# Six transformer layers twice over, on one core: the attention's weighted sum with the values as weights, and a new order of all engines

## The chip, the cores and the metric

The kernel runs on one core of one Trainium2 chip. The metric is the device time of one launch in microseconds, the median of several runs. A core has TensorE (matrix multiplication, writes to PSUM only), VectorE, ScalarE, GpSimd (which reaches SBUF, not PSUM), a SyncE queue that issues the transfers, and 16 DMA engines. In the profile they are PE (with PEld for its weight loads), DVE, ACT, POOL and SP.

## The reference, cut to what matters

The program is a residual chain of four phases on a tensor of 4 x 512 tokens by 128 features: a retention attention, a stack of six layers, an RWKV-like mixer, and the same stack again. The change touches the stack alone, which runs twice. All is float32. One layer of it, cut down:

```python
def attn_layer(x, Wqkv, qs, ksc, Wo):          # 16 heads of 64, windows of 32
    q, k, v = split(x @ Wqkv)                  # 128 -> 3 x 1024
    q, k = l2norm(q) * qs, l2norm(k) * ksc     # then rotary tables with a scale
    sim = einsum('bhwie,bhwje->bhwij', bq, look(bk)) * QK_SCALE   # own and previous window: 64 keys
    attn = softmax(where(mask, -max, sim), -1)
    out = einsum('bhwij,bhwje->bhwie', attn, look(bv))
    return out.reshape(b, n, INNER) @ Wo       # 1024 -> 128
def ffn_layer(x, g, bln, W1, b1, W2, b2):
    a, gate = split(layernorm(x) * g + bln @ W1 + b1)   # 128 -> 2 x 341
    return a * gelu(gate) @ W2 + b2
```

Before each layer's parts half of the features are shifted by one token, and each part is added to its input.

## The kernel before, in words

`ffn_stack` works through 96 tiles in each run of the stack: six layers, four sequences (a *group* of four tiles is one sequence in one layer), 128 tokens a tile. With two runs there are 192 tiles and 48 groups. Work is software-pipelined by *slots*: in slot N each engine does, in an order written out by hand (`slot` of each engine's block), one step of several tiles. `at(3)` is tile N-3, `of(2)` is group G-2; T is N mod 4, and steps of a group stand in one of the four kinds of slot. Nothing schedules at run time: each engine issues in its order, and waits on counting semaphores (`wait`).

A tile goes through these steps. GpSimd stages its 128x128 input (`stage`). TensorE projects six chunks of 512 columns, q0, q1, k0, k1 (8 heads each) and v0, v1 (`project`). VectorE multiplies q and k by the rotary tables out of PSUM (`rotate`, two instructions a chunk), ScalarE squares them (`square`) for the norms, GpSimd adds the two products (`rope`) and multiplies by the inverse norm (`unit`). TensorE transposes each of the four chunks (`turn`, 4 transposes), ScalarE copies them out (`keep`). `scores` are 2 x 32 small matmuls. VectorE adds the mask and takes the maximum (`mask_max`), GpSimd subtracts it (`off_max`), ScalarE takes the exponential (`exponent`). TensorE transposes these (`turn_probs`), ScalarE copies them (`probs_out`), and `weigh` multiplies them with the values: the transposed probabilities are the weights, 64 rows by 32 columns, and the values with a column of ones beside them are streamed, 65 columns. So a sum of each row of probabilities comes out beside each head. VectorE inverts it and multiplies (`norm_heads`), TensorE transposes the head outputs (`turn_heads`), ScalarE copies them (`heads_out`), and `project_out` multiplies by Wo. The feed-forward part follows by group (`center`, `variance`, `up` six times, `down`).

The values need a copy on the way: the small matmuls read each window's 64 keys from partitions of their own, so SyncE's queue copies `v_nat` into `v_w` by ten transfers a tile (`spread_values`). It also loads the next layer's weights, `w_o` and the feed-forward weights into single buffers after their last use.

PSUM has eight banks: two for projections (`proj`), two for what is transposed (`turnb`), two for scores, two for the head outputs (`bank_o`, shared by both halves of a tile). A table `PROJ` says which of a pair each step takes, and before each use TensorE waits for whoever read the bank last.

## Time and profile before

| | |
|---|---|
| median of 3 runs | 4020.71 us (4018.29 to 4024.47) |
| profiled execution | 4021.16 us, span 4019.4 us |
| PE | 3741.4 us, 93% |
| PEld | 2395.6 us, 60% |
| DVE | 3244.5 us, 81% |
| ACT | 2451.0 us, 61% |
| POOL | 2261.0 us, 56% |

The span is the time from the first to the last instruction of the profiled execution; the rest of its time lies around it. Busy shares are averages over all phases; the two stacks fill some 3530 us of the span.
### The profile page before, as it was taken

How to read it: one execution, taken by the hardware profiler on the slowest of the kernel's cores; microseconds unless marked ns; L12 is line 12 of the kernel's file. 1: busy time of each engine (PE TensorE's matmuls, PEld its weight loads, DVE VectorE, ACT ScalarE, POOL GpSimd, SP SyncE). 2: the span in 40 equal slices, each digit the busy share in tenths (PEclk: the TensorE clock that was granted, in tenths of full speed). 3: DMA queues.
4: the chain of work that ended last, by engine and by line, in shares of the span. 5: the costliest groups of instructions: out<-in, count | busy, mean ns of one | idle time of the engine just before them, and what ended most of it. 6: DMA issues, size and time to landing. Idle time of an engine off the chain costs nothing. (4 is left out here: it accounts for less than half of the span.)

```text
span 4019.4 us, 159581 instructions
## 1 busy us (share of the span) xinstructions
PE 3741.4 (93%) x63216; PEld 2395.6 (60%) x63216; DVE 3244.5 (81%) x11527; ACT 2451.0 (61%) x4337; POOL 2261.0 (56%) x2172
## 2 busy tenths in 40 slices
PE   6899999999999999987698599999999999999997
PEld 3466666666666666652465356666666666666664
DVE  6788888887888888864899688888887888888884
ACT  2467676665767676663422257676666667676674
POOL 1566666665666666643000166666666666666662
PEclk9899999999999999997799699999999999999998
DMA  1222322322323222210000132232322322332221
GB/s 56 76 72 63 79 74 76 84 67 68 82 64 77 75 66 72 72 45 15 1 0 6 33 82 65 71 84 67 79 76 61 80 76 63 81 76 71 70 64 38
DMA packets 170275, 254.12 MB, mean 63 GB/s; under 512 B 36544, under 2 KB 67264, under 8 KB 169408
## 3 DMA queue, kind: packets, MB, share of 16 engines
q1 hardware_dynamic: 169536, 243.87, 23.6%
q8 instruction: 512, 8.39, 0.9%
q14 instruction: 227, 1.86, 0.2%
HBM read 38.21 MB, written 1.05 MB: 10 GB/s over the span
## 5 line engine op out<-in xcount | busy, mean ns | idle before, releaser
L574 PE MATMUL stack_proj<-stack_w_qkv,stack_xs 128*128 128x512 f32 x2304 | 1191.5, 613 | 73.5 <-POOL stack_xs L1205 46.0
L1213 POOL TENSOR_TENSOR stack_roped<-stack_rot_c,stack_rot_s 128x512 f32<-128x512 f32 x768 | 972.9, 1275 | 355.4 <-DVE stack_rot_s L1036 355.4
L1223 POOL TENSOR_TENSOR stack_roped<-stack_roped,stack_rnorm 128x512 f32<-128x512 f32 x768 | 813.1, 1069 | 199.4 <-DVE stack_rnorm L1068 199.4
L1231 POOL TENSOR_TENSOR stack_s_m<-stack_s_m,stack_smax 128x512 f32<-128x512 f32 x384 | 400.6, 1043 | 595.8 <-DVE stack_smax L1079 595.8
L1034 DVE TENSOR_TENSOR stack_rot_c<-stack_proj,rot_tables 128x512 f32<-128x512 f32 x768 | 527.7, 687 | 231.8 <-PE stack_proj L574 225.5
L1079 DVE CUSTOM_DVE_ANT_0 stack_s_m<-stack_bank_s,band 128x64 f32<-128x64 f32 x3072 | 476.1, 220 | 158.4 <-PE stack_bank_s L597 149.7
L574 PEld LDWEIGHTS stack_proj<-stack_w_qkv,stack_xs 128*128 128x128 f32 x2304 | 369.2, 192 | 310.3 <-issue 141.3
L1045 DVE TENSOR_REDUCE stack_ssq<-stack_sq 128x8 f32<-128x512 f32 x768 | 520.5, 678 | 18.3 <-issue 4.3
L873 ACT ACTIVATE stack_sq<-stack_proj 128x512 f32<-128x512 f32 x768 | 460.7, 600 | 110.7 <-DVE stack_rot_s L1036 109.8
L1036 DVE TENSOR_TENSOR stack_rot_s<-stack_proj,rot_tables 128x512 f32<-128x512 f32 x768 | 521.8, 679 | 0.0
L582 PEld LDWEIGHTS stack_turn<-ident,stack_roped 128*128 128x128 f32 x3072 | 362.6, 141 | 224.3 <-issue 204.3
L582 PE MATMUL stack_turn<-ident,stack_roped 128*128 128x128 f32 x3072 | 471.3, 276 | 2.7 <-ACT stack_k_t L899 1.4
L916 ACT ACTIVATE stack_s_m<-stack_s_m 128x512 f32<-128x512 f32 x384 | 242.3, 631 | 369.3 <-POOL stack_s_m L1231 369.3
L643 PEld LDWEIGHTS stack_proj<-stack_o_t,stack_w_o 128*128 128x128 f32 x3072 | 374.5, 193 | 92.3 <-issue 90.8
L643 PE MATMUL stack_proj<-stack_o_t,stack_w_o 128*128 128x128 f32 x3072 | 377.3, 276 | 0.9 <-issue 0.9
L597 PEld LDWEIGHTS stack_bank_s<-stack_k_t,stack_q_t 64*32 64x32 f32 x24576 | 268.8, 105 | 179.3 <-issue 179.0
L907 ACT COPY stack_v_nat<-stack_proj 128x512 f32<-128x512 f32 x384 | 223.9, 583 | 209.5 <-PE stack_proj L574 198.9
L621 PE MATMUL stack_bank_o<-stack_v_w,stack_p_t 64*32 64x65 f32 x24576 | 336.4, 225 | 1.8 <-ACT stack_p_t L923 1.8
L597 PE MATMUL stack_bank_s<-stack_k_t,stack_q_t 64*32 64x64 f32 x24576 | 332.4, 224 | 1.2 <-issue 1.1
L664 PE MATMUL stack_proj<-stack_x_c,stack_w 128*128 128x512 f32 (+1 forms) x576 | 319.8, 638 | 14.4 <-ACT stack_x_c L962 6.2
L621 PEld LDWEIGHTS stack_bank_o<-stack_v_w,stack_p_t 64*32 64x32 f32 x24576 | 273.0, 105 | 94.1 <-issue 93.6
L899 ACT COPY stack_k_t<-stack_turn 128x512 f32<-128x512 f32 x384 | 224.9, 586 | 158.7 <-PE stack_turn L582 154.4
(256 smaller groups left out, 5227.4 us busy)
## 6 DMA issues: line engine op xcount, KB each, us to landing
stack_v_w<-stack_v_nat SPq DMA_DIRECT2D x1152, 130.0 KB
stack_v_w<-stack_v_nat SPq DMA_DIRECT2D x768, 65.0 KB
stack_w_qkv<-table_ffn_qkv SPq DMA_DIRECT2D x192, 96.0 KB, 2.3
stack_w_o<-table_ffn_wo SPq DMA_DIRECT2D x12, 512.0 KB, 4.7
stack_w<-table_ffn_w SPq DMA_DIRECT2D x12, 384.0 KB, 3.6
stack_w<-table_ffn_w SPq DMA_DIRECT2D x12, 192.0 KB, 3.1
x_outer<-L_attn_a_X SPq DMA_DIRECT2D x4, 256.0 KB, 7.0
ret_xpos<-table_xpos SPq DMA_DIRECT2D x1, 1024.0 KB, 6.4
```

The source lines that it names most:

```text
L574: pe.matmul(bank[:, :], xs[:, T, :], w_qkv[:, g.half, col:col + 512], start=True, stop=True).then_inc(done["proj_" + c], 1)
L582: last = pe.transpose(bank[:, P * n:P * (n + 1)], roped[:, CHUNKS.index(c), T % 2, P * n:P * (n + 1)], ident[:, :])
L597: last = pe.matmul(bank_s[j][WINDOW * n:WINDOW * (n + 1), 64 * hp:64 * hp + 64], q_t[rows, T % 2, hp, WINDOW * n:WINDOW * (n + 1)], k_t[ro ...
L621: last = pe.matmul(bank_o[WINDOW * n:WINDOW * (n + 1), gp, m * (HD + 1):(m + 1) * (HD + 1)], p_t[64 * gp:64 * gp + 64, j, m, WINDOW * n:WI ...
L643: last = pe.matmul(bank[:, 0:P], w_o[:, n, :], o_t[:, T % 2, n, :], start=n == 0, stop=n == PAIRS - 1)
L873: act.activation(sq[:, i % 2, :], proj[PROJ["p_" + c][T]][:, :], ACT.Square).then_inc(done["squared_" + c], 1)
L1034: dve.tensor_tensor(rot_c[:, i % 2, :].rearrange("p (h d) -> p h d", h=8), src.rearrange("p (h d) -> p h d", h=8), cosine, ALU.mult)
L1036: dve.tensor_tensor(rot_s[:, i % 2, :].rearrange("p (h f d) -> p h f d", h=8, f=2), src.rearrange("p (h f d) -> p h f d", h=8, f=2)[:, :, ...
L1045: dve.tensor_reduce(ssq[:, T % 2, i, :], sq[:, i % 2, :].rearrange("p (h d) -> p h d", h=8), AX.X, ALU.add).then_inc(done["summed_" + c], 1)
L1079: last = dve.tensor_tensor_reduce(s_m[:, T % 2, j, hp, :], bank_s[j][:, 64 * hp:64 * hp + 64], mask[:, first:first + 2 * WINDOW], 1.0, LOW ...
L1213: pool.tensor_tensor(roped[:, i, T % 2, :], rot_c[:, i % 2, :], rot_s[:, i % 2, :], ALU.add).then_inc(done["roped_" + c], 1)
L1223: pool.tensor_tensor(r, r, rnorm[:, T % 2, i, :].unsqueeze(2).broadcast_to([P, 8, HD]), ALU.mult).then_inc(done["united_" + c], 1)
```

## The change

What it does, in five parts.

1. **Values stationary.** In `weigh` the values are now the weights, 64 rows by 64 columns, and the transposed probabilities are streamed, 32 columns. As many matmuls as before, 32 for each half of a tile. The result comes out with the features on partitions, as `project_out` wants it, so `turn_heads` goes; `heads_out` copies from `bank_o` directly.
2. **Probabilities divided first.** The ones beside the values go. VectorE sums the exponentials (`sum_probs`) and inverts (`invert`), and GpSimd multiplies the probabilities (`scale_probs`) before they are transposed; `norm_heads` goes.
3. **Ring of four PSUM banks.** `proj` and `turnb` become `work`, four banks; each step takes the bank of table `BANK`, shifted by the sequence's number (`+ g.row`).
4. **A new order on every engine.** The lags are longer: the values are projected at lag 3 (before: 0 and 1), `weigh` stands at lag 5 (2), `project_out` at lag 6 (3), and the feed-forward part of a group ends in slot 2 of lag 3 (slot 3 of lag 2).
5. **Weights a layer ahead.** `w_o`, `w_1`, `w_2` and `vec` have two halves, and the next layer's are loaded during this one.

```diff
-        proj = [ps("proj0"), ps("proj1")]
-        turnb = [ps("turn0"), ps("turn1")]
+        work = [ps(f"work{n}") for n in range(4)]
-        w_o = sb("w_o", [P, PAIRS, DIM])
+        w_o = sb("w_o", [P, 2, PAIRS, DIM])
-        v_w = sb("v_w", [P, 2, 4, 8, HD + 1])
+        v_w = sb("v_w", [P, 2, 4, 8, HD])
-            "wo": (1, 1, 1, 1),
+            "wo": (0, 3, 1, 0),
...
@@ layer_loads
-                    if n == 1 and not first:
-                        sp.wait_ge(done["pe_wo"], 16 * layer + tile0)
-                        load_wo(layer)
-                    if n == 6 and not first:
-                        sp.wait_ge(done["x_set"], 4 * layer + x0)
-                        load_mlp(layer)
+                        if n == 4:
+                            sp.wait_ge(wo_in, 16 * layer + 16 * (layer0 + 1))
+                            if not first:
+                                sp.wait_ge(done["pe_wo"], 16 * layer + tile0)
+                            load_wo(layer + 1)
+                        if n == 11:
+                            ...
+                            load_mlp(layer + 1)
@@ turn_probs, weigh
-                wait(pe, f"exped{j}", t)
+                wait(pe, f"prob{j}", t)
-                for m in range(4):
-                    for gp in range(2):
-                        for n in range(4):
-                            last = pe.matmul(bank_o[WINDOW * n:WINDOW * (n + 1), gp, m * (HD + 1):(m + 1) * (HD + 1)],
-                                             p_t[64 * gp:64 * gp + 64, j, m, WINDOW * n:WINDOW * (n + 1)],
-                                             v_w[64 * gp:64 * gp + 64, T % 2, n, 2 * m + j, :], start=True, stop=True)
+                for half in range(2):
+                    for n in range(4):
+                        for odd in range(2):
+                            for gp in range(2):
+                                m, at = 2 * half + odd, P * half + WINDOW * n
+                                last = pe.matmul(bank_o[HD * odd:HD * (odd + 1), gp, at:at + WINDOW],
+                                                 v_w[64 * gp:64 * gp + 64, T % 2, n, 2 * m + j, :],
+                                                 p_t[64 * gp:64 * gp + 64, j, m, WINDOW * n:WINDOW * (n + 1)],
+                                                 start=True, stop=True)
-            def turn_heads(t, T, g, j, bank):
-                ...
@@ heads_out
-                act.copy(o_t[:, T % 2, 4 * j:4 * j + 4, :],
-                         turnb[PROJ[f"ot{j}"][T]][:, :].rearrange("p (g n) -> p g n", g=4)
+                act.copy(o_t[:, T % 2, 4 * j:4 * j + 4, :].rearrange("p (g h) n -> p g h n", g=2),
+                         bank_o[:, :, 0:2 * P].rearrange("p g (h n) -> p g h n", h=2)
                          ).then_inc(done[f"ot_set{j}"], 1)
@@ norm_heads goes
-                dve.reciprocal(inv[:, j, :, :].unsqueeze(3), heads[:, :, :, HD:HD + 1]).then_inc(done[f"inv{j}"], 1)
-                dve.tensor_tensor(o_n[:, j, :, :, :], heads[:, :, :, 0:HD], ...
+                dve.tensor_reduce(psum_p[:, j, :], s_m[:, T % 2, j, :, :], AX.X, ALU.add
+                                  ).then_inc(done[f"summed_p{j}"], 1)
...
+                dve.reciprocal(inv[:, j, :], psum_p[:, j, :]).then_inc(done[f"inv{j}"], 1)
@@ scale_probs, on GpSimd
+                wait(pool, f"inv{j}", t)
+                s = s_m[:, T % 2, j, :, :]
+                pool.tensor_tensor(s, s, inv[:, j, :].unsqueeze(2).broadcast_to([P, 8, 2 * WINDOW]), ALU.mult
+                                   ).then_inc(done[f"prob{j}"], 1)
```

Two places of the new order. The first is TensorE's, in a slot without feed-forward matmuls at its end: before, from the second projection of k to the last scores (L574 `project`, L582 `turn`, L631 `turn_heads`, L621 `weigh`, L597 `scores`).

```order
L574 MATMUL stack_proj<-stack_w_qkv,stack_xs 128x512
L631 MATMUL stack_turn<-ident,stack_o_n 128x128 x4
L621 MATMUL stack_bank_o<-stack_v_w,stack_p_t 32x65 x32
L582 MATMUL stack_turn<-ident,stack_roped 128x128 x4
L574 MATMUL stack_proj<-stack_w_qkv,stack_xs 128x512
L582 MATMUL stack_turn<-ident,stack_roped 128x128 x4
L597 MATMUL stack_bank_s<-stack_k_t,stack_q_t 32x64 x32
L631 MATMUL stack_turn<-ident,stack_o_n 128x128 x4
L574 MATMUL stack_proj<-stack_w_qkv,stack_xs 128x512
L597 MATMUL stack_bank_s<-stack_k_t,stack_q_t 32x64 x32
```

And now, to the end of the slot (L577 `project`, L611 `turn_probs`, L626 `weigh`, L600 `scores`, L585 `turn`):

```order
L577 MATMUL stack_work<-stack_w_qkv,stack_xs 128x512 x2
L611 MATMUL stack_work<-ident,stack_s_m 128x128 x4
L577 MATMUL stack_work<-stack_w_qkv,stack_xs 128x512
L626 MATMUL stack_bank_o<-stack_p_t,stack_v_w 64x32 x32
L600 MATMUL stack_bank_s<-stack_k_t,stack_q_t 32x64 x64
L585 MATMUL stack_work<-ident,stack_roped 128x128 x4
L611 MATMUL stack_work<-ident,stack_s_m 128x128 x4
```

The two groups of four transposes of head outputs are gone, the two halves of the scores stand together and right behind the second `weigh`, and what is weighed there is the tile five slots back.

The second place is GpSimd's whole slot: before (L1205 `stage`, L1231 `off_max`, L1223 `unit`, L1213 `rope`),

```order
L1205 COPY stack_xs<-stack_xst 128x128
L1231 TENSOR_TENSOR stack_s_m<-stack_s_m,stack_smax 128x512
L1223 TENSOR_TENSOR stack_roped<-stack_roped,stack_rnorm 128x512 x2
L444 REGISTER_ALU
L1213 TENSOR_TENSOR stack_roped<-stack_rot_c,stack_rot_s 128x512
L1223 TENSOR_TENSOR stack_roped<-stack_roped,stack_rnorm 128x512
L1213 TENSOR_TENSOR stack_roped<-stack_rot_c,stack_rot_s 128x512 x3
L1231 TENSOR_TENSOR stack_s_m<-stack_s_m,stack_smax 128x512
L1223 TENSOR_TENSOR stack_roped<-stack_roped,stack_rnorm 128x512
```

and now (L1192 `stage`, L1200 `rope`, L1218 `off_max`, L1226 `scale_probs`, L1210 `unit`):

```order
L1192 COPY stack_xs<-stack_xst 128x128
L1200 TENSOR_TENSOR stack_roped<-stack_rot_c,stack_rot_s 128x512 x2
L1218 TENSOR_TENSOR stack_s_m<-stack_s_m,stack_smax 128x512
L1226 TENSOR_TENSOR stack_s_m<-stack_s_m,stack_inv 128x512
L1218 TENSOR_TENSOR stack_s_m<-stack_s_m,stack_smax 128x512
L442 REGISTER_ALU
L1200 TENSOR_TENSOR stack_roped<-stack_rot_c,stack_rot_s 128x512 x2
L1210 TENSOR_TENSOR stack_roped<-stack_roped,stack_rnorm 128x512
L1226 TENSOR_TENSOR stack_s_m<-stack_s_m,stack_inv 128x512
L1210 TENSOR_TENSOR stack_roped<-stack_roped,stack_rnorm 128x512 x3
```

Two multiplications a tile are added (L1226), each between what VectorE inverts and what TensorE transposes; `stage` stands first and is followed by the `rope` of the tile before.

## Rows read from the trace of the kernel before

**Rows 1.** Busy time by engine over four successive slots: columns, and their sum.

```profile
core 0: us, PE busy (x) PEld busy (x) DVE busy (x) ACT busy (x) POOL busy (x), PEclk, DMA share, GB/s
...
sum 68.90, PE 67.88 PEld 44.20 DVE 58.20 ACT 47.37 POOL 45.83; mean PE 16.97 PEld 11.05 DVE 14.55 ACT 11.84 POOL 11.46
```

**Rows 2.** TensorE timeline of one slot: start us, us, engine, line, form, count.

```profile
1009.61 0.86 PE L621 MATMUL stack_bank_o<-stack_v_w,stack_p_t 64*32 64x65 f32 x64
1010.41 0.65 PE L608 MATMUL stack_turn<-ident,stack_s_m 128*128 128x128 f32 x4
...
1012.52 0.60 PE L631 MATMUL stack_turn<-ident,stack_o_n 128*128 128x128 f32 x4
1012.96 1.02 PE L664 MATMUL stack_proj<-stack_x_c,stack_w 128*128 128x512 f32 x2
...
1015.20 1.02 PE L574 MATMUL stack_proj<-stack_w_qkv,stack_xs 128*128 128x512 f32 x2
1016.06 0.60 PE L582 MATMUL stack_turn<-ident,stack_roped 128*128 128x128 f32 x4
...
1018.34 0.60 PE L631 MATMUL stack_turn<-ident,stack_o_n 128*128 128x128 f32 x4
1018.78 1.02 PE L574 MATMUL stack_proj<-stack_w_qkv,stack_xs 128*128 128x512 f32 x2
1019.73 0.86 PE L597 MATMUL stack_bank_s<-stack_k_t,stack_q_t 64*32 64x64 f32 x64
1020.52 1.13 PE L664 MATMUL stack_proj<-stack_x_c,stack_w 128*128 128x512 f32 x2
```

**Rows 3.** The same of a slot at 900 us, around the transposed head outputs.

```profile
900.86 0.60 PE L631 MATMUL stack_turn<-ident,stack_o_n 128*128 128x128 f32 x4
901.39 1.04 PE L621 MATMUL stack_bank_o<-stack_v_w,stack_p_t 64*32 64x65 f32 x64
...
905.03 0.66 PE L631 MATMUL stack_turn<-ident,stack_o_n 128*128 128x128 f32 x4
905.52 1.02 PE L574 MATMUL stack_proj<-stack_w_qkv,stack_xs 128*128 128x512 f32 x2
```

**Rows 4.** The same at 1041 us: the transposes of the probabilities and what follows.

```profile
1041.81 0.60 PE L608 MATMUL stack_turn<-ident,stack_s_m 128*128 128x128 f32 x4
1042.87 1.98 PE L574 MATMUL stack_proj<-stack_w_qkv,stack_xs 128*128 128x512 f32 x4 [0.46 <-POOL stack_xs L1205]
```

**Rows 5.** Weight loads of eight 8-column matmuls in the mixer, on the timeline.

```profile
2228.36 0.97 PEld L1925 LDWEIGHTS scan_bank<-scan_local,scan_seen 128*128 128x128 f32 x8 [0.88 <-issue]
```

**Rows 6.** Groups of instructions by line: TensorE and its weight loads.

```profile
L597 PE MATMUL stack_bank_s<-stack_k_t,stack_q_t 64*32 64x64 f32 x24576 | 332.4, 224 | 1.2 <-issue 1.1
L621 PEld LDWEIGHTS stack_bank_o<-stack_v_w,stack_p_t 64*32 64x32 f32 x24576 | 273.0, 105 | 94.1 <-issue 93.6
```

**Rows 7.** One line of the mixer: duration ns min/median/max of its loads.

```profile
L1925 PEld LDWEIGHTS scan_bank<-scan_local,scan_seen x8: 186/192/192, 2228.4 to 2229.1; 128*128 128x128 f32 x8
```

**Rows 8.** Groups by line: VectorE and GpSimd around the attention.

```profile
L1045 DVE TENSOR_REDUCE stack_ssq<-stack_sq 128x8 f32<-128x512 f32 x768 | 520.5, 678 | 18.3 <-issue 4.3 <-ACT stack_sq L873 0.6
L1092 DVE TENSOR_TENSOR stack_o_n<-stack_bank_o,stack_inv 128x512 f32<-128x512 f32 x384 | 265.4, 691 | 13.2
L1231 POOL TENSOR_TENSOR stack_s_m<-stack_s_m,stack_smax 128x512 f32<-128x512 f32 x384 | 400.6, 1043 | 595.8 <-DVE stack_smax L1079 595.8
```

**Rows 9.** TensorE timeline: first projection, first and last output projection, turning back.

```profile
107.18 1.22 PE L574 MATMUL stack_proj<-stack_w_qkv,stack_xs 128*128 128x512 f32 x1 [1.79 <-ACT stack_xst L1017]
...
154.49 2.05 PE L643 MATMUL stack_proj<-stack_o_t,stack_w_o 128*128 128x128 f32 x16
...
3971.22 1.95 PE L643 MATMUL stack_proj<-stack_o_t,stack_w_o 128*128 128x128 f32 x16
...
4008.58 1.91 PE L860 MATMUL stack_proj<-ident,stack_s_m 128*128 128x128 f32 x8 [2.59 <-DVE stack_s_m L1190]
```

**Rows 10.** Groups by line: the copy of the values, and what ended its waits.

```profile
L907 ACT COPY stack_v_nat<-stack_proj 128x512 f32<-128x512 f32 x384 | 223.9, 583 | 209.5 <-PE stack_proj L574 198.9 <-DMA stack_v_w<-stack_v_nat 8.8
```

More of the change, by code:

```diff
@@ L25 @@
 TILES = DEPTH * BATCH * SEQ // P
-N_CONSTS = 10
+N_CONSTS = 9
 RET_PARTS = ("q", "q_swapped", "k", "k_swapped")
@@ L642, in project_out @@
                 for n in range(PAIRS):
-                    last = pe.matmul(bank[:, 0:P], w_o[:, n, :], o_t[:, T % 2, n, :], start=n == 0, stop=n == PAIRS - 1)
+                    last = pe.matmul(bank[:, 0:P], w_o[:, g.half, n, :], o_t[:, T % 2, n, :], start=n == 0, stop=n == PAIRS - 1)
                 last.then_inc(done["pe_wo"], 1)
@@ L663, in up @@
                 n = min(P, HID - P * k)
-                pe.matmul(bank[0:n, :], w_1[:, 3 * (kind == "lin") + k, 0:n], x_c[:, :], start=True, stop=True
+                pe.matmul(bank[0:n, :], w_1[:, g.half, 3 * (kind == "lin") + k, 0:n], x_c[:, :], start=True, stop=True
                           ).then_inc(done[f"pe_{kind}{k}"], 1)
@@ L672, in down @@
                     n = min(P, HID - P * k)
-                    last = pe.matmul(bank[:, :], w_2[0:n, k, :], hid[0:n, k, :], start=k == 0, stop=k == 2)
+                    last = pe.matmul(bank[:, :], w_2[0:n, g.half, k, :], hid[0:n, k, :], start=k == 0, stop=k == 2)
                 last.then_inc(done["pe_down"], 1)
             def slot(N, T, G, at, of):
+                row = of(0).row
                 if T == 0:
-                    wait(pe, "squared_q1", N - 1)
-                    center(of(2), proj[0])
@@ new lines, in slot @@
+                    wait(pe, "pt_set0", N - 5)
+                    up(of(3), "lin", 1, work[(0 + row) % 4])
+                    wait(pe, "ot_set1", N - 6)
+                    weigh(*at(5), 0)
+                    wait(pe, "squared_k1", N - 1)
+                    turn(*at(2), "q0", work[(1 + row) % 4])
+                    wait(pe, "kept_k0", N - 2)
+                    turn(*at(2), "k1", work[(2 + row) % 4])
+                    wait(pe, "pt_set1", N - 5)
+                    turn(*at(2), "q1", work[(3 + row) % 4])
@@ new lines, in slot @@
+                    wait_group(pe, "hid1", G - 3)
+                    project(*at(0), "q0", work[(0 + row) % 4])
+                    wait(pe, "kept_q0", N - 2)
+                    project(*at(0), "k0", work[(1 + row) % 4])
+                    wait(pe, "kept_k1", N - 2)
+                    project(*at(3), "v1", work[(2 + row) % 4])
+                    wait(pe, "kept_q1", N - 2)
+                    project_out(*at(6), work[(3 + row) % 4])
+                    wait(pe, "squared_q0", N - 0)
@@ new lines, in slot @@
+                    project(*at(3), "v0", work[(0 + row) % 4])
+                    wait(pe, "squared_k0", N - 0)
+                    up(of(3), "gate", 2, work[(1 + row) % 4])
+                    wait(pe, "v_out1", N - 3)
+                    project(*at(0), "q1", work[(2 + row) % 4])
+                    wait(pe, "mid_set", N - 6)
+                    turn_probs(*at(4), 0, work[(3 + row) % 4])
+                    wait(pe, "v_out0", N - 3)
+                    project(*at(0), "k1", work[(0 + row) % 4])
@@ L851, in _ @@
                 for n in range(4):
-                    last = pe.transpose((proj + turnb)[s][:, P * n:P * (n + 1)],
+                    last = pe.transpose(work[s][:, P * n:P * (n + 1)],
                                         s_m[:, s // 2, s % 2, 2 * n:2 * n + 2, :], ident[:, :])
@@ L944, in center_out @@
                 wait_group(act, "pe_center", g)
-                wait_group(act, "pe_lin2", g.number - 1)
-                act.copy(x_c[:, :], proj[PROJ["ct"]][:, :]).then_inc(done["center_set"], 1)
+                for k in range(3):
+                    wait_group(act, f"pe_gate{k}", g.number - 1)
+                    wait_group(act, f"pe_lin{k}", g.number - 1)
+                act.copy(x_c[:, :], work[(BANK["ct"] + g.row) % 4][:, :]).then_inc(done["center_set"], 1)
             def inv_std(g):
@@ L1128, in finish @@
                 wait_group(dve, "pe_down", g)
-                bank = proj[PROJ["w2"]]
+                bank = work[(BANK["w2"] + g.row) % 4]
                 for rows, first in ((slice(0, 64), 0), (slice(64, P), 1)):
-                    last = dve.scalar_tensor_tensor(xst[rows, g.row, first:first + SEQ], bank[rows, :], vec[rows, 8:9],
+                    last = dve.scalar_tensor_tensor(xst[rows, g.row, first:first + SEQ], bank[rows, :], vec[rows, g.half, 8:9],
                                                     mshift[rows, g.pair, first:first + SEQ], ALU.add, ALU.add)
```

553 lines of the change are left out of this document (257 added, 296 removed), and 2 rows, old and new, of the table NAMES.

## The prediction

> **What bounds the kernel now.** I read the page's busy totals first, then the two stacks by windows, then one slot of TensorE instruction by instruction, then who makes it wait. Over four successive slots, one of each kind, the clock is full and TensorE is busy 67.88 of 68.90 us, so a slot takes 17.23 us and TensorE has 0.26 us of it free; VectorE is busy 14.55 us a slot, ScalarE 11.84, GpSimd 11.46 [rows 1]. The stack is TensorE-bound, and there are 192 slots of this sort. The reader is to see in the timeline that each row starts when the one before has issued: two passes of a projection start 0.86 us ahead of what follows, four transposes 0.44 us [rows 2]. So what counts is the issue time of TensorE's list, not a wait. The one wait that repeats: in two of the four kinds of slot the transposes of the probabilities take 1.06 us to the next start instead of 0.44, since the projection behind them waits for GpSimd's staged input [rows 2, 4]. The transfers hold nobody up: the copy of the values into `v_nat`, which also waits for the spreading of the tile before, lost 8.8 us to DMA in the whole run [rows 10].
>
> **The change part by part.** I count microseconds a slot and multiply by 192; the sum is made against the profiled execution, 4021.2 us, which is within 0.5 us of the median of the runs, 4020.7.
>
> *Transposes of head outputs removed.* Two groups of four a slot. Start to next start they take 0.44 and 0.44 in one kind of slot [rows 2] and 0.53 and 0.49 in the other three [rows 3], on average 0.98. They are on TensorE's list: -0.98 x 192 = -188 us.
>
> *Fewer entries into the small matmuls.* A projection before a small matmul takes 0.95 to the next start, before another full matmul 0.86 [rows 2]: 0.09 an entry. Before there are four blocks of small matmuls a slot, now two (one `weigh` alone; `weigh`, `scores`, `scores` together): -0.18, -35 us. At its end a block drains: the last scores pass, 0.224 us long, starts 0.86 - 0.224 = 0.64 us after the first, and the next matmul only at 0.79 [rows 2, 6], a gap of 0.15. Between the two halves of the scores it goes: -0.15, -28 us.
>
> *The wait for the staged input.* 0.62 in two of four slots, 0.31 a slot. In the new order three projections stand well inside the slot, behind `weigh` and twelve transposes, and `stage` is GpSimd's first step. I let it go: -60 us. What is late next is in the fifth term.
>
> *Values as weights.* This is the term on which the sign hangs. `weigh` takes 0.80 us now for 64 passes [rows 2], twice a slot. The trace has no matmul of 64x64 weights, so I bound it. What loading costs is seen where almost nothing is streamed: eight 8-column matmuls with 128-column weights have their loads start over 0.97 - 0.19 = 0.78 us, seven steps of 0.111 us [rows 5, 7]; 0.87 ns a column, 56 ns for 64 columns. Streaming costs 0.43 us per 512 columns [rows 2], 0.84 ns a column, 27 ns for 32. A load runs under another pass's streaming. An array of 128x128 holds eight tiles of 64x32 and four of 64x64; if each loads and streams by itself, a tile has 8 passes now, each 65 columns streamed over a 32-column load, 55 ns, 0.44 us; afterwards 16 passes, each bound by its load, 16 x 56 = 0.89 us. With the 0.15 us of draining that gives 0.59 (measured 0.80, so 0.2 lies in issuing) and 1.04. Lower bound: nothing but what streams counts, and it halves: 0.65. Upper bound: the loads of one row half go one behind the other, 32 x 56 ns + 0.15 = 1.93. Between: load and stream in series in each tile, 16 x 83 ns + 0.15 = 1.47. I take 1.10, near the load row, with a little of today's issue time on top: +0.30 twice a slot, +115 us. Each 0.1 us more or less is 38 us.
>
> The Trainium skill's "TensorE: Matmul & The Clock Gate", section "LDWEIGHTS (loading the stationary operand)", says that a load's time goes by the columns, not the rows, at 1.2 columns a ns; that is 53 ns for 64 columns and would make the term 16 x 53 ns + 0.15 = 1.0 us instead of 1.10, 38 us less in all. The row of 0.111 us for 128 columns agrees with it, and it speaks against the change, since the number of weight columns doubles. "TensorEngine Tiling (Array Packing)", sections "Available Configurations" and "When to Use Tiling", counts the same eight and four tiles, and for a side of 32 advises to make that side stationary, as the kernel does before; no row here shows 64x64, so this rule is weighed as the first rival.
>
> *Divided first.* VectorE: two multiplications out of PSUM of 0.69 go, two sums of 0.68 come [rows 8], the reciprocals stay: nothing. GpSimd: two multiplications of the shape of `off_max`, 1.04 each [rows 8]: 11.46 + 2.09 = 13.5 us a slot, under TensorE's 16.4. The chain exponent, sum, invert, scale, transpose crosses four engines, but the lag of one slot from `exponent` to `turn_probs` covers it. Hidden; if the cover were gone, it would cost up to the free time that GpSimd lacks, third rival. ScalarE: the same number of copies, nothing.
>
> *Ring, order, new waits.* With 13.5 to 14.6 us of work on two engines in a slot of 16.4, in-order waits can't all vanish. TensorE waits 0.26 a slot now with VectorE at 84%; it would be at 89%. I take +0.20 a slot for new ones, +38 us; the ends are 0 and 0.9, the last being what the slots would take if nothing were gained.
>
> *Longer lags.* Filling, first projection to first `project_out`, takes 47.3 us for three slots; from the last `project_out` to turning back 37.4 us [rows 9]. With six slots ahead of `project_out` the work is the same, but three more thin slots run by latency at each end; their work is missing from the others. The feed-forward part ends in slot 106 instead of 103. I take 10 us a stack, +20 us (ends 0 and 60).
>
> *Weights ahead, room for the transfer, 64 instead of 65 columns:* no wait of the trace is theirs, so 0. That is the part of the change that does not pay.
>
> Sum: -188 -35 -28 -60 +115 +38 +20 = -138, 4021 - 138 = 3883 us.
>
> **The rivals.** *First, slower: half as many tiles, each twice as long.* The place is `weigh`; the price is 64 passes that don't overlap as four independent tiles should. With load and stream in series (1.47 each) the sum is -138 + 0.37 x 384 = +4, 4025 us; doubling today's 0.65 and keeping the draining gives 1.45 and the same. With loads one behind the other in each row half (1.93) it is -138 + 0.83 x 384 = +181, less the 38 of waits, which a slower TensorE absorbs: 4164 us. The sign turns at 1.45 us. For it: the load row, and that 0.80 is more than eight independent tiles would take (0.59). Against: today's 32-column loads, 28 ns each by the same rate, would take 64 x 28 = 1.8 us one behind the other, and 0.9 in two halves, and all of `weigh` takes 0.80. Between 1.3 and 1.55: 10%; above: 14%.
>
> *Second: `weigh` stays at 0.80.* If issuing 64 passes is the limit, it is the limit afterwards too. The scores, 64 columns against 65 and otherwise the same, take 0.79 [rows 2], which fits both. Then TensorE needs 15.6 a slot, and VectorE at 14.55 of it (93%) makes it wait: -311 + 20 + 38 + 50 more = -203, 3818 us. 25%.
>
> *Third: another bound in the place of TensorE.* VectorE and GpSimd have their steps between TensorE's twice a slot; GpSimd can't start `unit` before VectorE's norm, and VectorE writes that only after `mid`, which waits for `project_out`. From there GpSimd has five steps, 5.2 us, before the slot's end. If this closes a loop a microsecond too long, it costs 1.05 instead of 0.20: 3883 + 163 = 4046 us. Against: counted along the rows, each of these has 2 us to spare. 9%.
>
> **How the numbers follow.** The forecast has 42% (its own range 3820 to 3950), the second rival 25%, the first 24%, the third 9%. A measurement of this kernel tells 0.2%, 8 us, from no change. Faster: nearly all of the forecast, the second rival, and half of the first's middle case, 71%. Same: 4%. Slower: 25%. The range: the lower end is a `weigh` of 0.80 with few waits, 3780; the upper one takes in the third rival and part of the first, 4120. Below lie some 7%, above some 12%.
>
> **What would show it.** Right: no L631; `weigh` (L626) about 1.1 us start to next start; a slot near 16.4 us with TensorE busy; GpSimd near 13.5. A `weigh` at 0.8 or at 1.5 and more shows the second or the first rival at once. Slots longer than TensorE's list, with waits on `prob`, `united` or `squared`, show the third. Fill and drain: six slots to the first `project_out`, in some 80 us. Wrong would be that a wait on `v_in` or on weights had hidden gains, or that VectorE, not TensorE, is busy throughout.

## The result and the profile after

The changed kernel takes 3952.57 us (median of four runs, 3945.82 to 3964.79) against 4021.49 us: a ratio of 0.9832, interval 0.9806 to 0.9858. That is 69 us gained, half of the 138 forecast and well outside the spread of the runs. The profiled execution took 3964.79 us, the longest of the four, so its sum is made over 56 us, from 4021.2.

The same windows as in [rows 1], four successive slots of the changed kernel:

```profile
core 0: us, PE busy (x) PEld busy (x) DVE busy (x) ACT busy (x) POOL busy (x), PEclk, DMA share, GB/s
921.20:942.02 20.82, 18.95 (x322) 12.21 (x321) 16.50 (x59) 12.41 (x26) 13.76 (x14) 1.00 0.22 53
942.02:957.63 15.61, 15.50 (x313) 10.74 (x312) 13.11 (x55) 12.19 (x21) 13.27 (x14) 1.00 0.29 71
957.63:973.73 16.10, 14.52 (x311) 10.27 (x310) 14.01 (x56) 9.78 (x21) 13.43 (x14) 1.00 0.30 73
973.73:988.95 15.22, 15.22 (x313) 10.50 (x312) 14.04 (x56) 11.41 (x20) 13.28 (x14) 1.00 0.27 64
sum 67.75, PE 64.20 PEld 43.73 DVE 57.66 ACT 45.80 POOL 53.73; mean PE 16.05 PEld 10.93 DVE 14.42 ACT 11.45 POOL 13.43
```

TensorE's busy time a slot fell from 16.97 to 16.05 us, near what the forecast wanted, but it is idle 3.55 us in these four slots where it was idle 1.02. Two slots have nearly all of it, 1.87 and 1.58 us, and the granted clock is 1.00 in all four. GpSimd went to 13.43 us, as worked out. The timeline of TensorE shows the two gaps. First a slot without one, then those two:

```profile
911.62 1.14 PE L626 MATMUL stack_bank_o<-stack_p_t,stack_v_w 64*64 64x32 f32 x64
912.69 1.58 PE L600 MATMUL stack_bank_s<-stack_k_t,stack_q_t 64*32 64x64 f32 x128
914.20 0.66 PE L585 MATMUL stack_work<-ident,stack_roped 128*128 128x128 f32 x4
...
917.26 1.53 PE L585 MATMUL stack_work<-ident,stack_roped 128*128 128x128 f32 x12
918.63 2.74 PE L577 MATMUL stack_work<-stack_w_qkv,stack_xs 128*128 128x512 f32 x6
...
927.81 1.14 PE L626 MATMUL stack_bank_o<-stack_p_t,stack_v_w 64*64 64x32 f32 x64
928.88 1.49 PE L600 MATMUL stack_bank_s<-stack_k_t,stack_q_t 64*32 64x64 f32 x116
932.24 0.33 PE L600 MATMUL stack_bank_s<-stack_k_t,stack_q_t 64*32 64x64 f32 x12 [1.87 <-issue]
...
963.59 1.36 PE L600 MATMUL stack_bank_s<-stack_k_t,stack_q_t 64*32 64x64 f32 x110
966.53 0.38 PE L600 MATMUL stack_bank_s<-stack_k_t,stack_q_t 64*32 64x64 f32 x18 [1.58 <-issue]
```

`weigh` is L626 now and takes 1.07 us start to start; `scores` is L600, both halves in a row, 1.51 us undisturbed. The gaps stand after pass 116 and pass 110 of the 128, inside a block where the code waits for nothing. The profile calls such a time "issue": the engine is idle, and no semaphore that the profile shows is what it waits for. Over the whole run this is now TensorE's largest wait. The waits of the changed kernel by who ended them (us, times, longest), and the groups that answer to [rows 6] and [rows 8]:

```profile
PE stack_bank_s L600 <- issue: 111.5, 81, 2.2
...
PE stack_work L577 <- ACT stack_sq L855: 21.0, 12, 2.5
...
PE stack_bank_o L626 <- issue: 14.3, 30, 1.3
```

```profile
L577 PE MATMUL stack_work<-stack_w_qkv,stack_xs 128*128 128x512 f32 x2304 | 1122.1, 603 | 36.3 <-ACT stack_sq L855 21.0 <-ACT stack_v_nat L889 4.7 <-issue 4.3
...
L626 PEld LDWEIGHTS stack_bank_o<-stack_p_t,stack_v_w 64*64 64x64 f32 x24576 | 405.4, 136 | 314.9 <-issue 308.8 <-ACT stack_o_t L913 3.1 <-DVE stack_mshift L1091 2.6
L1226 POOL TENSOR_TENSOR stack_s_m<-stack_s_m,stack_inv 128x512 f32<-128x512 f32 x384 | 400.8, 1044 | 9.4 <-DVE stack_inv L1081 9.4
...
L600 PE MATMUL stack_bank_s<-stack_k_t,stack_q_t 64*32 64x64 f32 x24576 | 322.2, 225 | 112.0 <-issue 111.5
...
L1073 DVE TENSOR_REDUCE stack_psum_p<-stack_s_m 128x8 f32<-128x512 f32 x384 | 259.4, 676 | 1.1 <-ACT stack_s_m L898 0.9
```

The same scores had 1.2 us of idle time before them in the kernel before [rows 6]; they have 112.0 now, with the same number of instructions of the same length. The wait for GpSimd's staged input, which [rows 4] shows once, is gone. The new sum (676 ns) and product (1044 ns) are as long as taken.

At the ends of the stack, answering to [rows 9]:

```profile
107.35 1.98 PE L577 MATMUL stack_work<-stack_w_qkv,stack_xs 128*128 128x512 f32 x4 [1.80 <-ACT stack_xst L1001]
...
187.35 1.95 PE L640 MATMUL stack_work<-stack_o_t,stack_w_o 128*128 128x128 f32 x16
...
3923.86 2.02 PE L640 MATMUL stack_work<-stack_o_t,stack_w_o 128*128 128x128 f32 x16 [0.89 <-DVE stack_hid L1109]
...
3952.20 3.63 PE L842 MATMUL stack_work<-ident,stack_s_m 128*128 128x128 f32 x16 [2.59 <-DVE stack_s_m L1178]
```

The filling takes 80.0 us (forecast some 80), the draining 28.3.

The clock was 1.00 in the four slots above, but not everywhere. After a long gap it can fall:

```profile
271.19 1.54 PE L600 MATMUL stack_bank_s<-stack_k_t,stack_q_t 64*32 64x64 f32 x125
274.67 0.30 PE L600 MATMUL stack_bank_s<-stack_k_t,stack_q_t 64*32 64x64 f32 x3 [1.93 <-issue]
```

```profile
268.00:276.10 8.10, 6.17 (x210) 4.53 (x209) 6.43 (x26) 3.78 (x8) 7.56 (x8) 1.00 0.22 50
276.10:282.90 6.80, 6.80 (x80) 4.90 (x79) 3.33 (x22) 2.46 (x7) 3.26 (x4) 0.50 0.39 99
```

In the middle of the two stacks (without the first 100 and the last 60 us of each) the clock falls to 0.50 (1.2 instead of 2.4 GHz) 18 times in the changed kernel, 78 us in all, each time 2.0 to 3.5 us after a step that was 1.9 us or more too long had begun; in the kernel before it does so twice, 14 us in all. Summed over the steps that are not stalls themselves (the term is defined below), these stretches cost 21 us against 2. By this estimate the gaps cost some 20 us beyond their own length.

Two numbers of my own working are used below. A **stall** is a step from one TensorE start to the next that is over 150 ns longer than the median step of its kind (same pair of lines, the one it starts in and the one it leads to); its excess over that median is summed over both stacks, whatever caused it. A stall inside a line has both its ends there. This gives somewhat more than the profile's idle time: 132 us inside L600 (97 stalls), 23 inside L626, 276 in all with the waits for other engines, against 107 in the kernel before, of which 3 lay in its scores. The **undisturbed slot** is the tenth percentile of the slots' lengths, taken in each of the four kinds and averaged: 15.95 us, before 17.14.

### The profile page after: what moved, and what is told of

The parts are those of the page before. It is cut to its first block and busy times, and to the rows that moved or that the text cites. A ratio compares the mean times of both kernels' runs of the same rounds, so it can differ in the third digit from the quotient of the medians.

```text
span 3963.0 us, 156885 instructions
## 1 busy us (share of the span) xinstructions
PE 3592.3 (91%) x61680; PEld 2388.6 (60%) x61680; DVE 3253.2 (82%) x11525; ACT 2372.4 (60%) x4337; POOL 2634.9 (66%) x2556
## 3 DMA queue, kind: packets, MB, share of 16 engines
q8 instruction: 497, 8.14, 0.9%
## 5 line engine op out<-in xcount | busy, mean ns | idle before, releaser
L1200 POOL TENSOR_TENSOR stack_roped<-stack_rot_c,stack_rot_s 128x512 f32<-128x512 f32 x768 | 966.3, 1273 | 420.9 <-DVE stack_rot_s L1020 420.9
L577 PE MATMUL stack_work<-stack_w_qkv,stack_xs 128*128 128x512 f32 x2304 | 1122.1, 603 | 36.3 <-ACT stack_sq L855 21.0
L1210 POOL TENSOR_TENSOR stack_roped<-stack_roped,stack_rnorm 128x512 f32<-128x512 f32 x768 | 784.6, 1043 | 175.9 <-DVE stack_rnorm L1052 175.9
L1018 DVE TENSOR_TENSOR stack_rot_c<-stack_work,rot_tables 128x512 f32<-128x512 f32 x768 | 518.3, 675 | 259.7 <-PE stack_work L577 256.5
L855 ACT ACTIVATE stack_sq<-stack_work 128x512 f32<-128x512 f32 x768 | 451.2, 598 | 367.7 <-DVE stack_rot_s L1020 367.6
L577 PEld LDWEIGHTS stack_work<-stack_w_qkv,stack_xs 128*128 128x128 f32 x2304 | 396.6, 193 | 335.1 <-issue 323.7
L626 PEld LDWEIGHTS stack_bank_o<-stack_p_t,stack_v_w 64*64 64x64 f32 x24576 | 405.4, 136 | 314.9 <-issue 308.8
L1020 DVE TENSOR_TENSOR stack_rot_s<-stack_work,rot_tables 128x512 f32<-128x512 f32 x768 | 522.0, 680 | 0.0
L1218 POOL TENSOR_TENSOR stack_s_m<-stack_s_m,stack_smax 128x512 f32<-128x512 f32 x384 | 421.2, 1097 | 114.9 <-DVE stack_smax L1063 113.5
L626 PE MATMUL stack_bank_o<-stack_p_t,stack_v_w 64*64 64x32 f32 x24576 | 452.1, 222 | 15.3 <-issue 14.3
L585 PE MATMUL stack_work<-ident,stack_roped 128*128 128x128 f32 x3072 | 436.0, 283 | 18.9 <-issue 13.9
L600 PE MATMUL stack_bank_s<-stack_k_t,stack_q_t 64*32 64x64 f32 x24576 | 322.2, 225 | 112.0 <-issue 111.5
L1226 POOL TENSOR_TENSOR stack_s_m<-stack_s_m,stack_inv 128x512 f32<-128x512 f32 x384 | 400.8, 1044 | 9.4 <-DVE stack_inv L1081 9.4
L585 PEld LDWEIGHTS stack_work<-ident,stack_roped 128*128 128x128 f32 x3072 | 343.7, 143 | 94.5 <-issue 66.4
L640 PE MATMUL stack_work<-stack_o_t,stack_w_o 128*128 128x128 f32 x3072 | 374.4, 275 | 3.6 <-issue 1.9
L600 PEld LDWEIGHTS stack_bank_s<-stack_k_t,stack_q_t 64*32 64x32 f32 x24576 | 275.5, 105 | 142.5 <-issue 133.3
```

The costliest lines, as they stand in the source:

```text
L577: pe.matmul(bank[:, :], xs[:, T, :], w_qkv[:, g.half, col:col + 512], start=True, stop=True).then_inc(done["proj_" + c], 1)
L585: last = pe.transpose(bank[:, P * n:P * (n + 1)], roped[:, CHUNKS.index(c), T % 2, P * n:P * (n + 1)], ident[:, :])
L600: last = pe.matmul(bank_s[j][WINDOW * n:WINDOW * (n + 1), 64 * hp:64 * hp + 64], q_t[rows, T % 2, hp, WINDOW * n:WINDOW * (n + 1)], k_t[ro ...
L626: last = pe.matmul(bank_o[HD * odd:HD * (odd + 1), gp, at:at + WINDOW], v_w[64 * gp:64 * gp + 64, T % 2, n, 2 * m + j, :], p_t[64 * gp:64 ...
L640: last = pe.matmul(bank[:, 0:P], w_o[:, g.half, n, :], o_t[:, T % 2, n, :], start=n == 0, stop=n == PAIRS - 1)
L1018: dve.tensor_tensor(rot_c[:, i % 2, :].rearrange("p (h d) -> p h d", h=8), src.rearrange("p (h d) -> p h d", h=8), cosine, ALU.mult)
```

## Experiments

Theory A, formed from these rows: TensorE runs out of instructions. In the 2.6 us of `weigh` and `scores` it issues 192 passes, each a load and a matmul, 384 instructions, some 150 a microsecond; a projection has 4 in 0.86 us, four transposes 8 in 0.44. The transfers of instructions to the core are on record in packets of 16.4 KB (497 packets, 8.14 MB). TensorE has 126,681 instructions on record, so that is 64 bytes an instruction and 256 instructions a packet. One packet starts at 930.04 us, beside the first gap. The rivals: a bank or a wait that the profile doesn't name, something of the second half of scores itself, or a cost of the longer lags or of the weights' earlier loads.

**Spread the short passes.** `weigh` first, k1's projection between the halves of scores; one slot kind shown, the others alike.

```
+ weigh(*at(5), 1)
  turn_probs(*at(4), 0, ...)
+ scores(*at(2), 0)
  project(*at(0), "k1", ...)
- center(...)                  # in the one slot kind of four that has it
- weigh(*at(5), 1)
- scores(*at(2), 0)
  scores(*at(2), 1)
+ center(...)
```

> The changed kernel with the second weigh and the two halves of the scores kept apart on TensorE: weigh before the transposes of the probabilities, first half of the scores before the second projection of k, second half behind it. Nothing else moves. Theory A, instruction supply: in the changed kernel the block of weigh and both halves of the scores (384 instructions, 2.6 us) runs ahead of the transfers that bring TensorE's instructions (16 KB, 256 instructions, about 2 us from start to use), and 131 us are lost inside blocks of scores at places where no wait stands. Spread out, no 256 instructions run in under 2 us, so those stalls go nearly wholly; two more entries and ends of small blocks cost 2 x 0.2 us a slot, +70 us. Sum -60 to -90 against the changed kernel: 3865 to 3895 us. Theory B, the stalls are waits for VectorE or ScalarE that the trace puts in the wrong place: they stay, and the entries add 70: about 4020 us.

Measured: 3961.06 us, ratio 0.9841 (0.9825 to 0.9857). The stalls did go, 132 to 22 us in L600 and 23 to 0.3 in L626, but the time didn't fall. The undisturbed slot grew by 0.86 us to 16.81 (165 us over 192 slots, where the expectation had 70), and in 44 slots a wait came up that the changed kernel doesn't have. `variance` waits there for ScalarE's square of q1, whose bank it takes; ScalarE makes that square right behind center's, and no half of scores stood between `center` and `variance` any more:

```profile
PE stack_work L654 <- ACT stack_sq L855: 52.8, 44, 1.3
...
PE stack_bank_s L600 <- issue: 8.7, 22, 1.0
```

So the stalls went as A says, and neither forecast of the time came true, on account of my own order. The same order with center ahead of the second half:

> As the spread order (weigh, turn_probs, first half, k1, second half, center: 3961 us), but with center ahead of the second half, so that a half of scores again stands between center and variance. Theory A (the spread order lost on the slots with T=1 because variance waited for center's squares, about 1.35 us in 48 slots x 2 stacks of 24 each way, 65 us in all): 3961 - 65 = about 3895 us, 3880 to 3910. Rival B (the spread order lost by its two more entries into small-matmul blocks a slot, 192 x 0.3 to 0.5 us): 3945 to 3965 us, the slots with T=1 as long as the others either way.

Measured: 3906.65 us, ratio 0.9704 (0.9685 to 0.9722), 54 us below the first spread and in the range expected; its stalls in L600 are 19 us. The wait fell, by 35 us in the profile's rows. From the second `weigh`'s start to `variance`'s it takes 5.60 us instead of 6.72 (medians of 48), 54 us in all, which is the whole difference:

```profile
PE stack_work L654 <- ACT stack_sq L855: 17.5, 44, 0.5
...
PE stack_bank_s L600 <- issue: 9.7, 21, 1.0
```

**Only `weigh` apart.** One long projection between `weigh` and the two halves, which stay together.

```
  turn_probs(*at(4), 0, ...)
+ weigh(*at(5), 1)
  project(*at(0), "k1", ...)
  center(...)
- weigh(*at(5), 1)
  scores(*at(2), 0)
  scores(*at(2), 1)
```

> The changed kernel with the second weigh alone moved ahead of the second projection of k; the two halves of the scores stay together. Theory A: 256 instructions still run in 1.45 us, but a stall needs the border of a transfer to fall into the scores, and there is less before them: the stalls within scores fall from 131 us to about half; one more entry and end costs 0.2 us a slot, 40 us. About -25: 3925 us, between the changed kernel and e1. Theory B: +40, 3990 us.

Measured: 3874.87 us (3866.82 to 3879.75), ratio 0.9632 (0.9616 to 0.9648), 78 us under the changed kernel. The stalls fell by 124 us, to 152 in all, those in L600 to 39; the undisturbed slot is 0.2 us longer (192 x 0.19 = 37 us), since there is one entry into small matmuls more. The difference, 87, is near the 78 measured. A's forecast of 3925 took too little of the stalls away: it left half of those in L600, and 39 of 132 us stayed.

**`weigh` and the first half together, the second half apart** (turn_probs, weigh, first half, k1, center, second half).

> The four slots' order becomes turn_probs, weigh, first half of scores, project k1 (and center where it stands), second half of scores. The same blocks with as many entries into small-matmul work as in the version with weigh apart (3875 us). Theory A (the stalls come where many short instructions follow each other without a long matmul between, whatever they are): weigh and the first half make 128 short passes in a row, the second half 64 alone; stalls in L600 and L626 together stay at 30 to 70 us of the 155 us that the changed kernel has, the time is 3865 to 3895 us. Rival B (the stalls belong to the two halves of scores in a row, for their banks or their 64-column streams): with the halves apart the stalls in L600 fall under 10 us and the time goes to 3830 to 3850 us. Rival C (stalls don't depend on the order): 3950 us.

Measured: 3906.15 us, ratio 0.9713 (0.9697 to 0.973), 11 us above A's range. The stalls are 45 us in L600 and 4 in L626, in A's range; B, which wanted under 10, falls: the two halves need not be neighbours. What the time has on top is the wait of `variance` again, 17.3 us, and an end more than in the version with `weigh` apart, since the halves of scores are no longer joined.

**The other way: everything short together** (k1 and center, then turn_probs, weigh, scores, scores).

> The other way than the version with weigh apart: project k1 (and center) goes ahead of turn_probs, so that turn_probs, weigh, both halves of scores and the turn behind them follow each other with no long matmul between. One entry and one end of a small-matmul block a slot fewer: 192 x about 0.2 us = 35 to 40 us off the list. Theory A (stalls grow with the run of short instructions): the stalls in L600, L626 and L585 together rise from 169 us to 220 to 330 us, which is more than the list gives back; 3960 to 4030 us, and the undisturbed slot about 15.8 us. Rival B (stalls come once per pair of scores halves, whatever stands ahead): stalls stay at 169 and the time is 3915 us.

Measured: 3953.56 us, ratio 0.9829 (0.9804 to 0.9855), the same as the changed kernel. Both forecasts missed. The stalls in the three lines are 176 us, hardly more than 169: turn_probs has four wide transposes in 0.44 us, 8 instructions, few for its time. That is my reading; no run tests it. And nothing came off the list (undisturbed slot 16.0): the number of entries into *small* matmuls did not change, only whether a projection or a transpose stands ahead of one.

**In the kernel before: the halves of scores together.** No other part of the change.

```
- scores(*at(1), 0)            # several steps earlier in the slot
  ...
+ scores(*at(1), 0)
  scores(*at(1), 1)
```

> The kernel before the change with one thing moved: the first half of the scores stands right before the second, at the slot's end. Its list of TensorE gets shorter by one entry (0.09) and one end (0.15) of a small block a slot, 46 us. Theory A: 256 instructions now run in 1.45 us, which the trace of before never had, so stalls of up to 0.7 us appear inside the scores wherever a transfer's border falls there: 4000 to 4050 us, with the stalls seen within L597 in the trace. Theory B (no such thing as a supply of instructions to run out of): 3975 us and no stall within L597.

Measured: 4065.04 us, ratio 1.0105 (1.0088 to 1.0122), slower by 43 us, 15 above A's range. The scores, with 1.2 us of idle time before [rows 6], now wait 48.2:

```profile
PE stack_bank_s L597 <- issue: 48.2, 40, 2.3
PE stack_proj L574 <- POOL stack_xs L1205: 44.1, 109, 0.5
```

Stalls in the scores went from 3 to 57 us, all stalls from 107 to 192. Of the 43 us the scores have 28; the transposes of head outputs and the projections have 10 and 9 more, which this theory doesn't explain. Putting these blocks together makes the gaps without values as weights, four banks or longer lags.

**Half the instructions for the same streamed columns.** The rest as in the changed kernel; every second head pair is multiplied by the queries of the pair before it, so its values are others.

```
- for hp in range(4 * part, 4 * part + 4):
+ for hp in range(4 * part, 4 * part + 4, 2):
...
-   pe.matmul(bank_s[j][..., 64 * hp:64 * hp + 64], q_t[...], k_t[rows, hp, key:key + 64], ...)
+   pe.matmul(bank_s[j][..., 64 * hp:64 * hp + 128], q_t[...], k_t[rows, hp:hp + 2, key:key + 64], ...)
```

> scores makes half as many passes, each with 128 streamed columns instead of 64, in the same order of blocks: half of the passes' weight loads and matmuls go, the streamed columns stay (every second head pair is multiplied by the pair before it, so the attention's values are others). Theory A (the stalls are a want of instructions, counted in instructions): both halves stay at 1.3 to 1.5 us without the stalls, those in L600 fall from 132 us to under 20, those in L626 from 23 to under 15, the time is 3952 - 110 to 130 = 3820 to 3850 us. Rival B (the stalls come with streamed columns, PSUM or time in tiled mode, not with the number of instructions): L600 keeps over 80 us of stalls and the time stays at 3930 to 3955 us.

Measured: 3681.28 us (3680.52 to 3684.6), ratio 0.9153 (0.9138 to 0.9168). No slot of the stretch has a gap in L600; on its timeline:

```profile
920.76 1.14 PE L626 MATMUL stack_bank_o<-stack_p_t,stack_v_w 64*64 64x32 f32 x64
921.82 1.22 PE L600 MATMUL stack_bank_s<-stack_k_t,stack_q_t 64*32 64x128 f32 x64
...
923.93 0.60 PE L585 MATMUL stack_work<-ident,stack_roped 128*128 128x128 f32 x4
```

```profile
q8 instruction: 401, 6.57, 0.8%
```

The stalls in L600 fell from 132 to 4.5 us, in L626 from 23 to none, in all from 276 to 92, under those of the kernel before. 24,576 instructions fewer are 96 packets fewer (497 to 401), 256 in each, as worked out above. A's time was 150 us too high for two reasons: the block itself is shorter (1.087 us start to start, not the 1.3 to 1.5 expected, 192 x 0.42 = 80 us), and stalls went elsewhere too, 185 us in all. Together 265 of the 271 measured. With as many streamed columns and the same banks the gaps are gone, so neither makes them. The number of weight loads has halved with that of the instructions, and this run alone doesn't part the two.

The packets on record do. I took each of the 135 stalls inside L600 and L626 of the changed kernel and looked how long before TensorE went on the last packet of instructions had ended: in 131 of them 1.1 to 1.7 us (median 1.42), all stalls over 0.5 us among these. Of instants taken at random 9% lie so. The same holds for the nine stalls in the scores of the kernel before (1.34 to 1.52 us) and for 154 of 154 in the version with everything short together. So TensorE goes on at nearly the same time after its instructions have arrived: their supply ends each gap. The sizes fit too. In the 94 stalls over 0.5 us it takes 2.52 us (median) from the last packet's start until TensorE goes on, and 134 instructions (median) were still issued in that time, at 6.7 ns each 0.9 us. That leaves 1.6 us of idle time, and the median of these stalls is 1.65.

**`weigh` with half its weight columns** (32 of 64 loaded, half of each head's features left out, `bank_o` filled with zeros once at the start), and **with twice its stream** (64 columns of probabilities instead of 32, wrong windows added), to test the term on which the sign hung.

```
- bank_o[HD * odd:HD * (odd + 1), gp, at:at + WINDOW], v_w[..., 2 * m + j, :], ...
+ bank_o[HD * odd:HD * odd + 32, gp, at:at + WINDOW], v_w[..., 2 * m + j, 0:32], ...      # the first
+ bank_o[HD * odd:HD * (odd + 1), gp, at:at + 2 * WINDOW], v_w[..., :], p_t[..., 64 wide] # the second
```

> weigh loads 32 of its 64 weight columns per pass, with the same streams of 32 columns; half of each head's features are left out of the result. Theory A (weigh's pace is its weight loads, 64 columns each, two tiles side by side: 1.065 us per block of 64 passes): the block falls to 0.65 to 0.80 us, 384 blocks x 0.3 us = 100 to 150 us off if nothing else ends last, 3830 to 3880 us; the stalls for want of instructions may take part of it back, since the same number of instructions comes in less time. Rival B (the pace is set by something per pass, not by the columns loaded): 1.00 to 1.07 us and 3945 to 3965 us.

> weigh streams 64 columns of probabilities per pass instead of 32, with the same weight loads; the attention's result is another one (wrong windows are added). Theory A (each pass's stream lies beside the next pass's load, and the load is the longer): the block stays at 1.05 to 1.15 us, the time at 3945 to 3975 us. Rival B (load and stream come one after the other): a block of 64 passes grows by 64 x 32 columns at the clock, shared by two tiles, to 1.45 to 1.55 us, 384 x 0.4 = 150 us, 4090 to 4120 us.

Measured, one run each: 3880.84 and 3957.83 us. The same lines of the first, then of the second:

```profile
911.69 0.76 PE L626 MATMUL stack_bank_o<-stack_p_t,stack_v_w 64*32 64x32 f32 x64
912.38 1.53 PE L585 MATMUL stack_work<-ident,stack_roped 128*128 128x128 f32 x12
```

```profile
905.41 1.16 PE L626 MATMUL stack_bank_o<-stack_p_t,stack_v_w 64*64 64x64 f32 x64
906.50 1.56 PE L600 MATMUL stack_bank_s<-stack_k_t,stack_q_t 64*32 64x64 f32 x128
```

Half the load makes the block 0.69 us (median 0.72), twice the stream 1.09 against 1.07. The loads set `weigh`'s pace, the streams lie beside them. Each was run once, but the lengths of the blocks are medians of 384. Of the 130 us that the shorter loads take out, about 72 arrived: the same instructions in less time stall more (L600 132 to 171 us, L626 23 to 40).

**Weights loaded late again**, into single buffers, after their last use in the layer before.

```
- w_o[:, layer % 2, :, :]      # w_1, w_2 and vec alike
+ w_o[:, 0, :, :]
```

> The changed kernel with the weights of output projection and feed-forward part loaded as before the change: into single buffers, after their last use. As predicted, loading a layer ahead gains nothing by itself: the time stays within 10 us of the changed kernel. Rival: the new order needs it, because the last down of a layer and gain_bias of the next stand in the same slot, so ScalarE waits there for x_set and a transfer of 3 us or more, with its squares queued behind it, once a layer: 10 times 5 to 10 us, +50 to +100 us.

Measured: 3957.59 us (3945.03 to 3971.55), ratio 0.985 (0.9821 to 0.9879), the same as the changed kernel. Loading a layer ahead gains nothing here, as expected.

**The best version tried.** The version with `weigh` apart, with the slot's other `weigh` behind the three turns instead of ahead of them.

> The version with weigh apart (3875 us), and the slot's other weigh behind the three turns of queries and keys instead of ahead of them. Theory A (the stalls in L626 are those of that weigh, 23 us, since it follows the scores by only two turns and one long matmul): they fall under 8 us and the time to 3850 to 3865 us. Rival B (the later weigh makes project_out or the eviction of its banks late, the list's slack there being unknown): 3880 to 3920 us, with a new wait at L640 or at the second weigh.

Measured: 3868.19 us (3863.84 to 3879.54), ratio 0.9622 (0.9601 to 0.9644), 3 us above A's range. The stalls in L626 are gone, but those in the turns (L585) rose from 10 to 27 us: they moved to what comes next. Not to be told from 3874.87. Both beat the changed kernel by 2%.

## Why the prediction was half right

For each group of TensorE's list I summed the time from its first start to the next group's, over both stacks of either profiled run. The undisturbed lengths of `weigh` and of the scores are taken apart; what the groups have above them stands in the term of waits:

| Term of the sum | forecast | measured |
|---|---|---|
| transposes of head outputs | -188 | -191 |
| entries into small matmuls (all other groups, with their few stalls) | -35 | -42 |
| an end between the halves of scores (1.504 a pair for twice 0.789) | -28 | -14 |
| wait for the staged input (`turn_probs`, 255 to 190) | -60 | -65 |
| `weigh` 0.79 to 1.065, undisturbed | +115 | +105 |
| ring, order, new waits | +38 | +151: 126 in `scores`, 25 in `weigh` |
| longer lags | +20 | about +8, inside the rows above |
| sum | -138 | -57 before rounding; the profiled runs differ by -56 |

**Right:** that TensorE's list of issue times bounds the kernel, and four of its terms to within 10 us. Two more are 12 and 14 us off. The end between the halves of scores is one of these: 0.15 a pair was read off, and the pair got 0.074 shorter. (In the kernel before, with its halves together, the pair takes 1.437 us, 0.14 shorter; why it is longer in the new order no run shows.) The first rival (1.45 us or more) and the second (0.80) both fell with 1.065. The third, a closed loop of VectorE and GpSimd, shows nowhere: in the stacks TensorE's largest wait for another engine is 21 us in 12 places, at the fill. Divided first cost nothing; GpSimd has 13.43 us in a slot of 16.9. Lags: the mean slot in mid-stack fell by 0.34 us, 65 us over 192; the stacks lost 57, so the ends cost about 8.

`weigh` was bound by its loads, as the load row of 0.111 us for 128 columns [rows 5] said: half the columns take 0.72 us, twice the stream hardly more than before. The rule of the Trainium skill, "TensorE: Matmul & The Clock Gate", section "LDWEIGHTS (loading the stationary operand)", that a load's time goes by its columns, agrees with the two experiments; the estimate by its rate was 1.0 us, and the block took 1.065.

**Wrong:** the step "ring, order, new waits: I take +0.20 a slot, +38 us". It looked for a semaphore wait that would be late, and asked of each instruction only what it waits for. What came is 0.79 us a slot (151 us; the stalls inside these blocks alone rose by 152) without any wait for an engine or a transfer of data, and it came from the order itself: `weigh` and the two halves of scores, 2.6 us in a row in which TensorE issues an instruction every 6.7 ns, 256 of them in 1.7 us, while 2.5 us pass from the start of a packet of 256 until TensorE goes on. Of the same move the prediction counted the gain (entries and one end, -63 us) and not this price. The rows gave a hint that I passed over: the scores had their only idle time from "issue" [rows 6], so this was already a quantity of the kernel, at 1.1 us, with nothing to say how it grows. The upper end of the term, 0.9 a slot, would have covered 0.79, but it stood for waits on other engines; that the size fell inside it is luck. The forecast's own range ended at 3950, 3 us below what was measured, and the wide one reached further for the sake of rivals that did not come true.

What stays open: when exactly a stall comes. It doesn't come in every slot (97 of 192 have one in the scores), the place of those over 0.5 us wanders between passes 83 and 125 of the 128, and a longer row of short work (all together) hardly made more of them. The arrival of the packet ends a stall; what sets the time at which a packet starts was not tried.

## What to carry to other kernels

Short matmuls that stand in a row save entries and ends, but a row of some hundreds of them can outrun the supply of instructions; one projection between two such blocks was worth 78 us here. Look for idle time put down to "issue" inside a block of one line: it is no wait, and the cure is order or fewer, wider instructions. Before moving a step between others, ask which chain it was covering: ScalarE's squares between `center` and `variance` had their cover in a half of scores.

## What the hardware showed that I had not expected

- Of the 97 stalls inside the scores of the changed kernel 72 are over 0.5 us, the longest 2.4 us, and no pair of halves has two. TensorE goes on 1.1 to 1.7 us after the end of the last packet of instructions. 24,576 instructions fewer took exactly 96 such packets away.
- A gap has a second price: 18 times in mid-stack the granted clock fell to 0.50 for 3.4 to 10.2 us, always within 3.5 us of the start of a step that was 1.9 us or more too long. With `weigh` apart it fell 4 times, with half the instructions in the scores twice.
- 128-column streams over 32-column loads: 64 passes take 1.09 us, 128 passes with 64 columns 1.50. Twice as wide is cheaper by 28% for the same columns; both are lengths without stalls.
- A load of 64 weight columns is 136 ns on record (L626), one of 32 columns 105 to 108; the pace of the block goes by the columns all the same (1.07 against 0.72 us).
- The runs of one kernel spread with the mean granted clock: the changed kernel took 3945.82 us at 0.963 and 3964.79 at 0.959, and the version with weights loaded late 3945.03 at 0.964 and 3971.55 at 0.959. Which of the two drives the other no run shows.
